# Two chained cross-attention layers on one core: prologue, head sums and step order rebuilt

## The reference

```
# layer 0, 16 heads of 16
q = split(rmsnorm(x, gamma_q) @ Wq.T)
kn = rmsnorm(ctx, gamma_kv);  k = split(kn @ Wk.T);  v = split(kn @ Wv.T)
mask = |ctx_pos - index| <= 1
w = where(mask, square(relu(q k^T / sqrt(16))), 0)
x1 = x + (w / max(sum(w), EPS_DEN)) v @ Wo.T
# layer 1, one head, x1 as queries
q = gelu(x1 @ Wq + bq);  k = gelu(ctx @ Wk + bk);  v = gelu(ctx @ Wv + bv)
out = layernorm(softmax(q k^T) v @ Wf + bf + x1) * ln_gamma + ln_beta
```

## Time and profile before

| what | value |
|---|---|
| median of 3 runs | 351.77 us (351.51 to 351.79) |
| profiled execution | 351.55 us |
| its span, first to last instruction | 349.7 us |
| PE busy | 327.5 us (94%) |
| DVE busy | 307.4 us (88%) |
| ACT busy | 242.6 us (69%) |
| POOL busy | 174.2 us (50%) |
| moved by DMA | 38.48 MB, mean 110 GB/s |
| PE's share of the chain of work that ended last | 76% |

### The profile page before, as it was taken

One profiled execution on the slowest core, in us unless ns is written; L12 is line 12 of the kernel. 1 busy time (PEld: TensorE's weight loads), 2 busy tenths in 40 slices (PEclk: granted clock), 3 DMA queues, 4 the chain that ended last, 5 costly groups with the idle time before them and its releaser, 6 DMA issues.

```text
span 349.7 us, 5560 instructions
## 1 busy us (share of the span) xinstructions
PE 327.5 (94%) x1908; PEld 236.8 (68%) x1908; DVE 307.4 (88%) x486; ACT 242.6 (69%) x491; POOL 174.2 (50%) x202
## 2 busy tenths in 40 slices
PE   2989998999999999999999999999999999999980
PEld 1564676868676768686777767676868686767750
DVE  0789597799999999999999999999999999999766
ACT  3799434276959595959595968687786868685752
POOL 3815020023838393847474746474756656444514
PEclk9999999999999999999999999999999999999995
DMA  7957714812233232414141414141413232010103
GB/s 238 354 169 191 218 60 112 226 53 87 76 108 103 77 123 67 145 60 151 60 151 60 150 63 149 62 149 62 147 63 130 82 121 90 0 62 0 62 0 121
DMA packets 22347, 38.48 MB, mean 110 GB/s; under 512 B 2160, under 2 KB 8816, under 8 KB 22320
## 3 DMA queue, kind: packets, MB, share of 16 engines
q1 hardware_dynamic: 19344, 30.01, 27.1%
q0 software_dynamic: 2016, 7.34, 6.1%
q10 hardware_dynamic: 960, 0.79, 0.7%
HBM read 17.29 MB, written 8.39 MB: 73 GB/s over the span
## 4 chain that ended last, share of the span: by engine, by line
PE 76%; DVE 9%; ACT 5%; issue 4%; POOL 2%; DMA 1%; SPq 1%; ACTq 0%; POOLq 0%
PE ps L481 11%; PE ps L482 11%; PE ps L483 11%; PE ps L560 7%; PE ps L532 7%; PE ps L526 5%; PE ps L610 4%; PE ps L641 4%; PE ps L726 4%; PE ps L717 4%; PE ps L615 2%; PE ps L513 2%; DVE qkp L1240 1%; DMA x_ring<-xT 1%; DVE ps L1251 1%
## 5 line engine op out<-in xcount | busy, mean ns | idle before, releaser
L370 POOL TENSOR_TENSOR x_lo<-x_ring,x_hi 128x1024 fp32r<-128x1024 f32 x16 | 38.4, 2398 | 38.8 <-ACT x_hi L972 38.8
L1240 DVE TENSOR_TENSOR qkp<-ps,bufs 128x1024 f32<-128x1024 f32 x48 | 55.8, 1214 | 0.9 <-PE ps L526 0.8
L1048 ACT ACTIVATE xp_hi<-bufs 128x512 fp32r<-128x512 f32 x28 | 17.7, 633 | 45.5 <-DVE bufs L1320 45.5
L410 POOL TENSOR_TENSOR bufs<-bufs,lng_twice 128x1024 f32<-128x1024 f32 x14 | 33.7, 2406 | 27.1 <-ACT bufs L1010 25.0
L383 POOL TENSOR_TENSOR mean_gap<-stats 128x4 f32<-128x4 f32 x14 | 2.8, 198 | 71.7 <-DVE stats L1309 65.0
L1251 DVE TENSOR_TENSOR ps<-ps,wn 128x1024 f32<-128x1024 f32 x31 | 37.9, 1224 | 0.0
L412 POOL TENSOR_TENSOR bufs<-bufs,lnb_row 128x1024 f32<-128x1024 f32 x14 | 33.3, 2380 | 1.1
L560 PE MATMUL ps<-qkp,cst 128*32 128x512 f32 x192 | 30.7, 598 | 0.4 <-DVE qkp L1240 0.4
L560 PE MATMUL ps<-bufs,cst 128*32 128x512 f32 x64 | 30.5, 598 | 0.0
L976 ACT ACTIVATE bufs<-ps 128x512 f32<-128x512 f32 x32 | 19.2, 602 | 14.1 <-PE ps L483 14.0
L481 PE MATMUL ps<-x_hi,wh_q 128*128 128x512 f32 x64 | 26.8, 418 | 0.0
(11 more groups left out here) (248 smaller groups left out, 927.5 us busy)
## 6 DMA issues: line engine op xcount, KB each, us to landing
x_ring<-xT SPq DMA_DIRECT2D x16, 512.0 KB, 3.5
out<-bufs POOLq DMA_DIRECT2D x14, 512.0 KB, 3.4
idx_ring<-idx SPq DMA_DIRECT2D x16, 256.0 KB, 3.9
wkv_lo<-kv SPq DMA_DIRECT2D x32, 126.0 KB
kvs<-kv SPq DMA_DIRECT2D x30, 126.0 KB
vfd<-bufs SPq DMA_DIRECT2D x8, 256.0 KB, 3.9
qkp<-ctxT SPq DMA_DIRECT2D x2, 512.0 KB, 7.3
bufs<-ctx SPq DMA_DIRECT2D x2, 512.0 KB, 8.7
```

The lines of the kernel that those rows point to most:

```text
L370: G.tensor_tensor(x_lo[:, :, :], x_ring[:, e % RING, :, :], f32_view(x_hi[:, :, :]), ALU.subtract).then_inc(xl_ready, 2)
L410: G.tensor_tensor(zo, zn, lng_twice[:, :].unsqueeze(1).broadcast_to([P, TT, D]), ALU.mult).then_inc(zg_ready, 1)
L1240: V.tensor_tensor(qk[:, s, :, :], ps[:, bank0:bank0 + 2, :], q0, ALU.mult).then_inc(qk_ready, 1)
```

## The change

**Head sums by token tile.** For each half g and each of four tiles of 128 tokens one product takes all three shifts (384 columns) and writes the 32 rows of that tile. After it three transposes instead of four lead to the weights by token; relu on 384 columns without bias.

**The floor from rows of x.** x is passed a second time, untransposed. SP loads a batch's rows (512 KB) at the end of the step before; ACT squares them, one tile each, with an accumulator; DVE's clamp takes the floor from SBUF.

**Order of a step.** PE: first half of the projection ahead of picked values UP, second half behind; picked values CENTRE ahead of the lower keys. DVE: a residual ahead of `attend` UP; the second residual and the first remainder ahead of `attend` DOWN, the second remainder behind; `attend` CENTRE ahead of the last key product; a remainder L1291 between clamp and reciprocal. ACT: the square between the two roundings.

**Prologue.** PE multiplies zeros three times before its first data; the context's squares of half 0 are made from the columns (ACT, one instruction) and summed by PE; one load of context rows (512 KB) goes; ACT instead of DVE rounds the folded weights; `keys1(0, 1)` moves behind the first head sums and `keys1(1, 1)` behind `values1(0, ...)`; `final_values` 2 and 3 move to either side of the first transposes of step 3; POOL tries its power once early and waits for `wkv_ready` before its first low part of x; DVE prepares the query weights after its first keys and values.

```diff
+            def load_rows(i):
+                if i > 0:
+                    sp.wait_ge(floor_ready, TT * i)
+                sp.dma_start(x_rows, x[i].rearrange("(j p) d -> p j d", p=P)).then_inc(rows_in, 16)
...
             context_columns(0)
-            context_rows(0)
             weight(raw["k0"], wk0T, wkv_in)
...
             context_columns(1)
-            context_rows(1)
+            context_rows()
+            load_rows(0)
             weight(raw["v1"], wv1, wv1_in)
...
                 if e is not None and e >= 2:
                     shifted(e)
+                if e is not None:
+                    load_rows(e)
...
             context_scale(0)
+            pool.wait_ge(wkv_ready, 2)
             split_x_lo(0)
...
+            def context_sums():
+
+                pe.wait_ge(ctx_sq_ready, 1)
+                pe.wait_ge(ones_set, 1)
+                for t in range(4):
+                    for c in range(DC):
+                        last = mm(ps[:, SUMS_BANK, t:t + 1], ctx_sq[:, c, t * P:(t + 1) * P], ones[:, 0:1], start=(c == 0), stop=(c == DC - 1))
+                last.then_inc(cms_mm, 1)
...
                 pe.wait_ge(qk_ready, 3 * a + 3)
-                pe.wait_ge(xsq_ready, a + 1)
                 for g in range(DC):
-                    for s in range(SHIFTS + 1):
-                        i = mm(ps[32 * s:32 * s + 32, 0, :], sum_sel[:, g if s < SHIFTS else 2, :],
-                               qk[:, s, g, :] if s < SHIFTS else xsq[:, g, :], start=(g == 0), stop=(g == DC - 1))
+                    for j in range(TT):
+                        i = mm(ps[32 * j:32 * j + 32, 0, 0:SHIFTS * P].rearrange("p (s t) -> p s t", s=SHIFTS), sum_sel[:, g, :],
+                               qk[:, :, g, j * P:(j + 1) * P], start=(g == 0), stop=(g == DC - 1))
                 i.then_inc(s_mm, 1)
...
+            pe.wait_ge(clear_set, 1)
+            for _ in range(3):
+                mm(ps[:, 1, :], s_sb[:, 0:P], s_sb[:, :], start=True, stop=True)
             pe.wait_ge(wk1_in, 16)
             pe.wait_ge(ctxT_in[0], 16)
             keys1(0, 0)
-            keys1(0, 1)
+            context_sums()
...
             head_sums(0)
+            keys1(0, 1)
...
+                if f == 1:
+                    pe.wait_ge(vf_copied, 1)
+                    final_values(2)
...
-                    for j in range(TT):
-                        i = nc.tensor.transpose(ps[:, 0, j * P:(j + 1) * P], s_sb[:, j * P:(j + 1) * P], ident)
+                    for s in range(SHIFTS):
+                        i = nc.tensor.transpose(ps[:, 0, s * P:(s + 1) * P], s_sb[:, s * P:(s + 1) * P], ident)
                     i.then_inc(sT_mm, 1)
-                if f == 0:
-                    keys1(1, 1)
+                if f == 1:
+                    pe.wait_ge(vf_copied, 2)
+                    final_values(3)
...
+                if b is not None:
+
+                    pe.wait_ge(oh_ready, 2 * b + 2)
+                    pe.wait_ge(ol_ready, 2 * b + 2)
+                    if b == 0:
+                        pe.wait_ge(w1_ready, 2)
+                    project(1)
                 if f is not None:
...
                     picked_values(f, UP, 4)
                 if b is not None:
-
-                    pe.wait_ge(oh_ready, 2 * b + 2)
-                    pe.wait_ge(ol_ready, 2 * b + 2)
-                    if b == 0:
-                        pe.wait_ge(w1_ready, 2)
-                    for i in (1, 0):
-                        for c in range(DC):
-                            product(ps[:, O0_BANKS[i], :], *weight("o0", c, i), o_hi[:, c, :], o_lo[:, c, :], c == 0, c == DC - 1, xp_mm)
+                    project(0)
...
-                if a is not None:
-                    pe.wait_ge(sum_ready, 2 * f + 1)
-                    picked_keys(a, DOWN, 0)
                 if f is not None:
...
                     picked_values(f, CENTRE, 2)
+                if a is not None:
+                    pe.wait_ge(sum_ready, 2 * f + 1)
+                    picked_keys(a, DOWN, 0)
...
             def square_x(a):
-                if a > 0:
-                    act.wait_ge(s_mm, a)
-                A(xsq, x_ring[:, a % RING, :, :], ACT.Square).then_inc(xsq_ready, 1)
+                act.wait_ge(rows_in, 16 * a + 16)
+                if a > 1:
+                    act.wait_ge(dcl_ready, a - 1)
+                for j in range(TT):
+                    A(x_rows[:, j, :], x_rows[:, j, :], ACT.Square, scale=FLOOR_SCALE,
+                      accum_out=floor[:, a % 2, j:j + 1]).then_inc(floor_ready, 1)
...
+                if b is not None:
+                    remainder(0)
+                if f == 1:
+                    copy_final_values(3)
...
-                    V.tensor_tensor(dcl[:, :, :], den[:, :, :], den_floor.broadcast_to([P, TT, H]), ALU.max).then_inc(dcl_ready, 1)
+                    dve.wait_ge(floor_ready, TT * f + TT)
+                    V.scalar_tensor_tensor(dcl[:, :, :], floor[:, f % 2, :].unsqueeze(2).broadcast_to([P, TT, H]), 16.0 * EPS_DEN * EPS_RMS,
+                                           den[:, :, :], ALU.add, ALU.max).then_inc(dcl_ready, 1)
+                if b is not None:
+                    remainder(1)
...
+                if b is not None:
+                    residual(1)
                 if f is not None:
...
                     attend(f, 0, UP, 4, att_flat(0))
                 if b is not None:
...
+                    residual(0)
+                    query_remainder(1)
                 if f is not None:
                     attend(f, 1, DOWN, 0, picked(0))
+                if b is not None:
+                    query_remainder(0)
...
                     multiply_keys(a, CENTRE, 2)
+                    multiply_keys(a, UP, 6)
+                if f is not None:
+                    attend(f, 2, CENTRE, 2, picked(2))
+                if a is not None and f is not None:
+                    multiply_keys(a, DOWN, 0)
```

More of the change, by code:

```diff
@@ L99, in xattn_pair @@
         bufs = sb("bufs", [P, 8, DC * T])
-        xsq, q0, xpT, q1T = (bufs[:, n, :].rearrange("p (c t) -> p c t", c=DC) for n in (0, 3, 4, 5))
+        q0, xpT, q1T = (bufs[:, n, :].rearrange("p (c t) -> p c t", c=DC) for n in (3, 4, 5))
+        x_rows = bufs[:, 0, :].rearrange("p (j d) -> p j d", j=TT)
+        floor = sb("floor", [P, 2, TT])
         zn, zo = (bufs[:, n, :].rearrange("p (j d) -> p j d", j=TT) for n in (6, 7))
@@ L642, in step, with project @@
                     i.then_inc(z_mm, 1)
-                if f is not None:
-                    if f == 0:
-                        pe.wait_ge(v1_copied, 2)
-                    if f == 1:
-                        for pair in range(2, 4):
-                            pe.wait_ge(vf_copied, pair - 1)
-                            final_values(pair)
-                        pe.wait_ge(vf_copied, 4)
-                    picked_values(f, UP, 4)
+                def project(i):
+                    for c in range(DC):
+                        product(ps[:, O0_BANKS[i], :], *weight("o0", c, i), o_hi[:, c, :], o_lo[:, c, :], c == 0, c == DC - 1, xp_mm)
                 if b is not None:
@@ L1258, in _ @@
             build_onehot(0)
+            dve.wait_ge(wq0_in, 16)
+            for c in range(DC):
+                V.tensor_scalar(w_hi["q0"][:, c, :], raw["q0"][:, c, :], vec[:, 0, c:c + 1], None, ALU.mult).then_inc(wq0_hi_ready, 1)
+            for c in range(DC):
+                dve.wait_ge(wq0_hi_ready, c + 1)
+                last = V.scalar_tensor_tensor(w_lo["q0"][:, c, :], raw["q0"][:, c, :], vec[:, 0, c:c + 1],
+                                              f32_view(w_hi["q0"][:, c, :]), ALU.mult, ALU.subtract)
+            last.then_inc(wq0_ready, 1)
             keys_values_remainder(1)
@@ L1287, in step, with remainder @@
                     copy_final_values(1)
+                    copy_final_values(2)
+                def remainder(g):
+                    dve.wait_ge(oh_ready, 2 * b + g + 1)
+                    V.tensor_tensor(o_lo[:, g, :], ps[:, TURN_BANKS[g], :], f32_view(o_hi[:, g, :]), ALU.subtract).then_inc(ol_ready, 1)
                 if b is not None:
[L1289 to L1291 removed]
+                    remainder(0)
+                if f == 1:
+                    copy_final_values(3)
                 if f is not None:
```

145 lines of the change are left out of this document (75 added, 70 removed).

## The result

The kernel after takes **357.67 us** (median of 4 runs, 356.47 to 358.28) against 351.72 for the kernel before beside it: ratio 1.0166, 95% interval 1.0138 to 1.0195. It is slower, by 6 us, where 349.45 and a gain were forecast; it lies outside the range (348.3 to 350.8), and outside the wider one that was given for 8 in 10. The profiled execution took 358.01, its span is 356.2 (before 349.7).

A forecast was written before the change was run, and what follows sets the result against it. A steady step was taken as bound by a loop: picked sum, PE's transposes through to score transposes, maxima, next sum. From 351.55 us, 1.9 for the prologue and 0.2 over 13 steps gave 349.45, range 348.3 to 350.8.

The forecast's parts named there:

- They land at about 42.5: Prologue: batch 1's rows, loaded behind the ln rows, land at about 42.5, putting centre keys at 46.0 against 46.13.
- The upper bound, 5 us: Prologue: rows landing in 5 us rather than 3.5 would leave a gain of 0.3 us.
- Steps 2 and 3: Prologue: one final-value product (1.7 us) moves into a wait; DOWN values of step 3 come at 63.0 instead of 64.89.
- The step, 18.13 to 18.18: Steady step: 0.55 us of PE work saved goes into waits of 0.3 and 0.2; -0.2 us over 13 steps.
- the walk: Steady step followed on the profile's clock: second remainder ready at 213.35, PE wanting it at 213.09, so waiting 0.26 to 0.3.
- rival 2: Second half of the queries: the held product costs up to 0.25 more; step 18.43, total 352.9; chance 0.13.
- Before PE asks for it: End of a step: the last key product, behind the attention product moved ahead of it, ends at 219.0, in time.
- Rival 1: Steady step: second remainder in time, loop tightens to 17.88; 3.9 us over 13 steps, total 345.8; chance 0.22.
- Rival 3: Prologue gives nothing, batch 1's rows being late and zeros not speeding PE; total 351.3; chance 0.13.
- Rival 4: Head sums: rounds stay at 0.43, costing no more than 0.1 a step, inside the forecast's range; no separate chance given.
- The zeros: Prologue: three products of zeros release PE's throttle during the load; four key passes take 1.7 us instead of 3.4.
- Head sums: Steady step: rounds of 0.32, 0.43 us less PE work, plus 0.12 for a transpose; not in the loop through L730.

The follow-up runs named there:

- ln_last: Kernel after with the two ln rows moved behind the load of batch 1's rows on SP's queue; 352.19 us, one run.
- keep_warm: Kernel after plus six discarded products of 512 columns while TensorE waits for batch 1's centre keys; 356.56 us, 1.0131 of before.
- rem_late_only: Kernel after with batch 1's rows loaded early and the third product's order as before; split projection and late second remainder stay; 349.85 us, 0.9950 of before.
- rem_first: Kernel after with both query remainders ahead of the product of the DOWN values on DVE; 358.07 us, 1.0167 of before.
- rows_early: Kernel after with the load of batch 1's rows put behind the fifth crossing instead of behind the ln rows; 350.73 us, 0.9968 of before.
- order_back: Kernel after with batch 1's rows loaded early and both new orders of a step put back as before; 346.10 us, 0.9848 of before.
- copies_wait: Kernel after with the four shifted copies of batch 2 held until batch 1's rows have landed; 355.96 us, one run.

## Why the prediction was wrong

Against its own clock the sum was off by 358.01 - 349.45 = 8.56 us: 5.9 before the first maxima (78.06, forecast 74.02 - 1.9 = 72.1), 2.9 in the steps (+2.7, forecast -0.2), -0.2 in the tail.

**"They land at about 42.5": the failing step.** The load was issued at 38.94 as put, and landed at 46.3. The 3.5 us is the median landing of another load, that of the columns of x, which in a steady step comes first; this one stood behind the ln rows, which the prediction itself named as ahead of it. Of the 3.9 us that were missing, 2.7 went with the ln rows (4.7 in ln_last); the other 1.2 are what a load of rows takes more in the other steps too (median 4.9), whether for its layout or for the shifted copies ahead of it is not shown. The upper bound, 5 us, rested on no row. Centre keys: 49.24 instead of 46.0, only 3.2 later, since squares and gelus took 2.9 where the sum has 3.5. In ln_last the squares start at 42.55, just as forecast, but by luck: the load was issued 1.1 us earlier and took 1.2 us longer than the 3.5. Centre keys follow at 45.46, DOWN values of step 3 at 62.94 (63.0 forecast).

**What was not in the sum at all: TensorE standing still.** The longer wait took the granted clock to its 1.2 GHz level for the products behind it, 2.0 us by keep_warm. In ln_last, where TensorE stands for 1.48 us ahead of the centre keys, the clock stays at 1.00. One delay was so paid one and a half times.

**Steps 2 and 3** were to bring 1.77 us between centre keys and maxima; at full clock they bring 27.89 - 26.87 = 1.02 (ln_last). Too much by 0.75. These three are 3.2 + 2.0 + 0.75 = 5.95, all of the start's miss.

**The step, 18.13 to 18.18: mechanism right, size short.** Everything up to the second remainder came as walked: its end 11.90 us behind the sum, 11.87 in the walk. The held product starts 0.15 behind that end, and the next one 0.30 behind it instead of 0.23; the walk left both out. PE loses 0.38 before the held product, not 0.26 to 0.3. The three, 0.03, 0.15 and 0.07, carry through to the transposes L769: 17.61 behind the sum, 17.36 at the least in the walk. That is rival 2's mechanism, the held product, at most of its price; its sum of 352.9 kept the forecast's prologue and so missed too.

**A second wait behind the first.** "Before PE asks for it" was true of the last key product and left out the CENTRE keys: their bank is asked for first. In the kernel after PE doesn't wait there, and its step is only 0.04 over that of rem_late_only, but it is why undoing the remainder alone (rem_first) gave nothing, against my own expectation.

**Rival 1, 17.88,** could not be had. The 0.19 us by which VectorE came late to the maxima was read as slack; it was the loop. With nothing late for PE the step is 18.08. **Rival 3** named the late rows, but at a price of the prologue's 1.9 us and with zeros that do nothing; the landing alone was worth 7.2 (78.06 against 70.88 in rows_early). **Rival 4** is out: the rounds took 0.32.

**The zeros.** Forecast by the spacing of 1.2 GHz and not by the granted clock of 1.00 that the windows of before show there. Four key passes took 1.79 us (6.18 to 7.97), where the spacing gave 3.4 without the zeros. The weight loads of the zeros themselves come 0.85 apart (from 2.46 to 5.02), those of the keys behind them 0.43, and the granted clock is given as 1.00 in all these windows: here the spacing told the level. The Trainium skill's rule ("TensorE: Matmul & The Clock Gate", Part 1), that activity releases the throttle, gave 1.7; the trace agrees with it, though no run leaves out the zeros alone.

**Head sums.** 0.32 a round was right (sixteen in 1.50 with the last one's tail, 1.92 before), and so was "not in the loop": with the transpose, the squares and the clamp together they give 0.09 a step, 18.17 to 18.08 (order_back). Squares on ACT, the clamp, one more load per step on SP: none shows as a cost in a step; in the kernel after ACT has done the squares by 103.3 and idles 1.2 us before the next rounding.

## What to carry to other kernels

A landing time holds only for the queue it was read on: list what is issued ahead, broadcast rows above all, and put the load that somebody waits for first. When a wait of TensorE grows, read the granted clock of the windows behind it before adding up. And before moving work within a tight loop, find the chain without a gap from milestone to milestone; two late values on one engine hide each other, so undo both before saying that either is free.

## What the runs showed of the hardware

The rows of batch 1, the same 512 KB on the same queue, took between 4.1 us (rows_early) and 7.4 us (the kernel after) to land; the DMA share was 0.79 with 117 GB/s in a window of copies_wait, where it took 6.1, and 0.93 with 288 GB/s in ln_last, where it took 4.7. TensorE's granted clock fell from 1.00 to 0.50 during a standstill of 5.15 us (the kernel after) and at the end of one of 3.78 us (copies_wait, 0.54 in the window from 48), and in the kernel after it was still 0.50 in the window from 52, with TensorE busy since 49.24; the Trainium skill, "TensorE: Matmul & The Clock Gate", Part 1, has it that the throttled state is the default and activity releases it, and the trace agrees: in keep_warm, with products running through the wait, it stayed at 1.00. A product held by a semaphore started about 0.15 us behind its releaser's end, and its whole spacing was 0.61 us instead of 0.23 (the kernel after, 108.80).
